# Mamba's ramp and drain: output weights rounded later, fewer idle matmuls, early choice in three parts, last y ahead of scoring

## What is computed

```python
x = x + attention(layernorm(x))          # 16 heads, sliding window of 128
x = x + moe(layernorm(x), gate, w1, w2)  # 8 experts, 2 of them for each row
x = x + mamba(layernorm(x))              # inner width 1024, 16 heads, state 128
x = x + moe(layernorm(x), gate, w1, w2)

def mamba(x):                            # the stage that is changed
    z, xBC, dt = split(x @ in_proj_w.T)
    xs, B, C = split(silu(causal_conv4(xBC) + conv_b))
    y = scan(xs * dt, A, B, C) + xs * D  # state carried over blocks of 64 rows
    y = y * silu(z)
    return (y / sqrt(mean(y * y) + 1e-5) * norm_w) @ out_proj_w.T

def moe(x):
    two best of softmax(x @ gate.T), renormalised; sum of silu(x @ g) * (x @ u) @ w2 over them
```

## Time and profile before

| | |
|---|---|
| times of three runs | 1614.23, 1621.25 and 1623.17 us, median 1621.25 us |
| profiled execution, its time and its span | 1608.78 us, 1607.1 us |
| PE busy in the span | 93%, at a mean granted clock of 0.972 |
| DVE, ACT, POOL busy | 57%, 45%, 38% |
| Mamba's first and last matmul | 738.78 us; 1304.38 us (a group of 1.88 us) |

### The profile page before, as it was taken

How to read it: one execution, slowest core, us unless ns; L and a number is a source line. 1 busy time by engine, 2 the same in 40 slices (tenths; PEclk the granted TensorE clock), 3 DMA queues, 4 the chain that set the end, 5 groups by cost and what they waited for, 6 DMA issues and landing times. The chain is left out here.

```text
span 1607.1 us, 34125 instructions
## 1 busy us (share of the span) xinstructions
PE 1493.9 (93%) x11983; PEld 1262.4 (79%) x12004; DVE 923.4 (57%) x2133; ACT 721.0 (45%) x1784; POOL 606.0 (38%) x473
## 2 busy tenths in 40 slices
PE   6999999999699999997799999999999779999996
PEld 5787887887478898895588787887887558999996
DVE  4677677776732234223687978878878762222221
ACT  3766666666222234333555644564546302333332
POOL 5655465465323334431222332233223403333342
PEclk9999999999799999998899999999999969999999
DMA  6364454463569877543001011010100138787753
GB/s 218 105 206 163 175 204 149 177 210 138 206 210 329 242 221 225 125 67 106 14 21 34 21 34 54 21 34 21 43 32 21 35 130 270 218 266 204 190 97 49
DMA packets 95917, 212.36 MB, mean 132 GB/s; under 512 B 7216, under 2 KB 7216, under 8 KB 94512
## 3 DMA queue, kind: packets, MB, share of 16 engines
q1 hardware_dynamic: 76736, 166.58, 29.7%
q0 software_dynamic: 17472, 40.90, 12.8%
q10 hardware_dynamic: 1584, 3.15, 0.5%
HBM read 136.94 MB, written 73.66 MB: 131 GB/s over the span
## 5 line engine op out<-in xcount | busy, mean ns | idle before, releaser
L1299 PE MATMUL bank<-ring,halves 128*128 x1872 | 332.0, 326 | 3.5 <-ACT halves L1139 3.5
L1299 PEld LDWEIGHTS bank<-ring,halves 128*128 128x128 f32 x1872 | 302.6, 188 | 10.6 <-issue 4.5
L499 POOL TENSOR_TENSOR arena<-arena 128x1024 f32<-128x1024 f32 x64 | 123.8, 1934 | 142.2 <-DVE arena L579 140.6
L1697 DVE SCALAR_TENSOR_TENSOR arena<-arena 128x256 f32<-128x256 f32 x240 | 128.4, 577 | 19.3 <-ACT arena L1916 16.5
L1593 POOL TENSOR_TENSOR arena<-arena 128x1024 f32<-128x1024 f32 x16 | 31.3, 1957 | 280.1 <-ACT arena L1970 240.8
L792 PE MATMUL bank<-arena 128*128 128x128 f32 x1024 | 125.0, 281 | 1.8 <-ACT arena L692 0.8
L711 ACT ACTIVATE arena<-arena 128x256 f32<-128x256 f32 x256 | 126.3, 499 | 0.0
L792 PEld LDWEIGHTS bank<-arena 128*128 128x128 f32 x1024 | 119.0, 195 | 7.7 <-issue 3.6
L1119 POOL DMA_INDIRECT out_dram<-arena x39 | 61.7, 1582 | 154.2 <-issue 90.8
L1119 POOL DMA_INDIRECT mid_rows<-arena x39 | 61.8, 1585 | 148.2 <-issue 94.3
L1139 ACT ACTIVATE halves<-bank 128x512 fp32r<-128x512 f32 x78 | 46.6, 597 | 157.2 <-PE bank L1282 157.2
(11 more groups left out here) (285 smaller groups left out, 3265.8 us busy)
## 6 DMA issues: line engine op xcount, KB each, us to landing
ring<-expert_halves SPq DMA_DIRECT2D x16, 4352.0 KB, 18.8
expert_halves<-expert_high SPq DMA_DIRECT2D x16, 1088.0 KB, 8.7
expert_halves<-expert_rest SPq DMA_DIRECT2D x16, 1088.0 KB, 10.8
arena<-in_w_dram SPq DMA_DIRECT2D x8, 1088.0 KB, 6.6
normalised_rows<-arena SPq DMA_DIRECT2D x33, 256.0 KB, 2.0
arena<-in_x_dram SPq DMA_DIRECT2D x32, 256.0 KB, 2.7
arena<-mid_rows SPq DMA_DIRECT2D x32, 256.0 KB, 2.8
w_in_raw<-in_in_w_dram SPq DMA_DIRECT2D x16, 290.0 KB, 6.6
```

Of the source, the lines that this page charges most:

```text
L499: nc.gpsimd.tensor_tensor(held, held, spread(rinv[:, HG * g:HG * g + HG], 2, 2 * P), ALU.mult)\
L1299: last = nc.tensor.matmul(bank[1 + 2 * par + part][:, 0:INTER], rows_parts[a][:, par, k * P:k * P + P], weights(at, b, (2 * k + part) * IN ...
L1697: last = nc.vector.scalar_tensor_tensor(out=slot[:, j], in0=cin[:, c, k:k + PAIR], scalar=taps[:, c, k:k + 1], in1=slot[:, j], op0=ALU.mul ...
```

## The change

Six edits, all of them in the order of work:

- TensorE's idle matmuls ahead of Mamba are 19 where they were 26; in the prologue ScalarE copies the fifth unit in ahead of the silu of the third.
- ScalarE makes the eight high parts of the output weights in turn 0 behind `conv_in(1, 0)`, no longer ahead of the turn; VectorE makes their rests behind `convolve(1, 0)`, no longer ahead of `own_out(0)`.
- `early_choice` is three calls, for tiles 0 to 5, 6 to 11, and 12 and 13. In Mamba they stand in the last turn behind `rest_of_y(13)`, behind `first_block(14)` and behind `rest_of_y(14)`. In attention all three stand where the one stood.
- In the last tile VectorE's work has an order of its own, `last_rows`: the y of tile 15 is made before tile 14 is scored.
- Tile 14's normalised rows get memory of their own (`keep_apart`), so that the y of tile 15 may be rounded first. The scoring products of tiles 14 and 15 both come behind the last projection on TensorE, in banks 1 and 2.
- 12 new idle matmuls stand between `early_rank` and `turn_y(15)`; the two halves of `spots` stand on either side of the last `put_out`.

```diff
     def early_rank(self, pe):
-        pe.wait_ge(self.early_both, 1)
+        pe.wait_ge(self.early_both, len(self.CHOICES) - 1)
...
         scored = Scoring(core, sem, xn_rows, scored_rows_at, scored_at)
+        scored.keep_apart(TILES - 2, xc_at)
...
+                if not front:
+                    dve.wait_ge(x_turned, TILES)
+                    sort.early_choice(link, 0)
                 mix(t)
                 first_block(t)
+                if not front:
+                    sort.early_choice(link, 1)
                 second_block(t)
-                if first:
-                    rest_of_w_out()
...
                 if front:
                     convolve(link, n, 0)
+                if first:
+                    rest_of_w_out()
...
+            def last_rows(link, t):
+                dve.wait_ge(scored.ready, t - 1)
+                sort.early_choice(link, 2)
+                mix(t)
+                first_block(t)
+                second_block(t)
+                put_out(t - 1)
+                own_out(t)
+                rows_done(link, t, 1)
+                dve.wait_ge(added, t)
+                scored.statistics(dve, link, xres)
+                scored.normalise(dve, t - 1, xres)
+                mean_of(t)
+                rest_of_y(t)
+                dve.wait_ge(z_made, 2 * TILES)
+                sort.early_spots(dve, link)
+                sort.spots(0, sort.EARLY, 0)
+                put_out(t)
+                dve.wait_ge(added, TILES)
+                scored.statistics(dve, link, xres)
+                scored.normalise(dve, t, xres)
+                scored.logits_out(dve, t - 1, bank[1])
+                last = sort.spots(0, sort.EARLY, 1)
+                scored.logits_out(dve, t, bank[2])
+                link(last)
...
                 act.wait_ge(y_turned, t + 1)
                 after(act, out_made, t)
-                after(act, scored.made, t)
-                after(act, scored.stored, 16 * t)
+                after(act, scored.made, min(t, TILES - 2))
+                after(act, scored.stored, 16 * min(t, TILES - 2))
...
                 if front:
                     conv_in(n, 0)
+                if not begun:
+                    high_of_w_out()
...
-            stay_busy(core, bank[7], 26)
+            stay_busy(core, bank[7], 19)
...
             sort.early_rank(pe)
+            stay_busy(core, bank[1], 12)
             turn_y(TILES - 1)
             project_high(TILES - 1)
             project_rest(TILES - 1)
-            pe.wait_ge(scored.xn_ready, TILES)
-            scored.turn(pe, TILES - 1, bank[7])
-            scored.product(pe, TILES - 1, bank[7])
+            scored.turn(pe, TILES - 2, bank[1])
+            scored.product(pe, TILES - 2, bank[1])
+            scored.turn(pe, TILES - 1, bank[2])
+            scored.product(pe, TILES - 1, bank[2])
```

More of the change, by code:

```diff
@@ L199, in __init__, with own_rows, keep_apart, xn @@
         self.made, self.ready, self.stored = sem("logits_made"), sem("logits_ready"), sem("out_xn_stored")
+    def own_rows(self, at):
+        xn, at = cut(self.core.arena, at, D)
+        return xn, cut(self.core.arena, at, KD, P)[0]
+    def keep_apart(self, n, rows_at):
+        self.apart, self.rows_apart = n, self.own_rows(rows_at)
+    def xn(self, n):
+        return (self.rows_apart if isinstance(n, int) and n == self.apart else self.own)[0]
+    def xnT(self, n):
+        return (self.rows_apart if isinstance(n, int) and n == self.apart else self.own)[1]
     def statistics(self, dve, link, x):
@@ L238, in product @@
         for k in range(KD):
-            last = self.nc.tensor.matmul(bank[:, 0:EXPERTS], self.xnT[:, k], self.core.gate[:, k],
+            last = self.nc.tensor.matmul(bank[:, 0:EXPERTS], self.xnT(n)[:, k], self.core.gate[:, k],
                                          start=(k == 0), stop=(k == KD - 1))
@@ L615, in step @@
                     dve.wait_ge(made, SORT_MADE)
-                    sort.early_choice(link)
+                    for part in range(3):
+                        sort.early_choice(link, part)
                 if front:
@@ L1422, in mamba @@
         bc.append(c)
+    xc_at = at
     xc, at = cut(arena, at, KY, PAIR)
@@ L1833, in turn @@
                 rest_of_y(t - 1)
+                if not front:
+                    last_rows(link, t)
+                    return
                 mix(t)
                 first_block(t)
-                if front:
-                    convolve(link, n, 2)
+                convolve(link, n, 2)
                 second_block(t)
-                if front:
-                    convolve(link, n, 3)
-                else:
-                    dve.wait_ge(z_made, 2 * TILES)
-                    sort.early_choice(link)
+                convolve(link, n, 3)
                 put_out(t - 1)
@@ L1876, in _ @@
                 turn(link, i, i % 2, first=(i == 0), front=(i < LAST))
-            sort.early_spots(dve, link)
-            mean_of(TILES - 1)
-            rest_of_y(TILES - 1)
-            for k in range(TOPK):
-                last = sort.spots(0, sort.EARLY, k)
-            link(last)
-            put_out(TILES - 1)
-            dve.wait_ge(added, TILES)
-            scored.statistics(dve, link, xres)
-            scored.normalise(dve, TILES - 1, xres)
-            scored.logits_out(dve, TILES - 1, bank[7])
         @block.scalar
@@ L1993, in decay, with high_of_w_out @@
                     last.then_inc(decays_ready, 1)
+            def high_of_w_out():
+                act.wait_ge(w_out_here, 16)
+                for k in range(KY):
+                    nc.scalar.activation(w_out_parts[0][:, k], w_out[:, k], ACT.Copy, scale=norm[:, k:k + 1])\
+                        .then_inc(w_out_high, 1)
             def turn(i, pp):
@@ L2054, in _ @@
             conv_in(0, 3)
+            conv_in(0, 4)
             conv_out(0, 2, 0)
-            conv_in(0, 4)
             conv_out(0, 3, 0)
```

43 lines of the change are left out of this document (20 added, 23 removed).

## The result

| | before | changed |
|---|---|---|
| median of 12 runs of each, taken beside one another | 1614.09 us | 1603.89 us |
| span of the profiled execution | 1607.1 us | 1605.1 us |
| busy: PE, DVE, ACT, POOL | 93, 57, 45, 38% | 93, 58, 45, 38% |
| mean granted clock | 0.972 | 0.972 |
| Mamba, from its first load to the mixture's first load | 569.34 us | 558.91 us |

The ratio is 0.992, with a 95% interval from 0.9901 to 0.9939. That is 12.9 us less (9.8 to 16.0); the forecast was 17.0 less. The ratio is not the quotient of the two medians in the table, which lie 10.2 us apart (0.9937); that value is inside the interval too.

The account below looks back on a forecast made before the run. TensorE, busy nearly all the time, was taken as the bound, so only its waits and low clock could pay. Terms -1.5 - 6.4 - 9.2 + 0.1 = -17.0 us took 1621.25 to 1604.3 us; range 1596 to 1611.

Parts of the forecast that it names:

- Idle matmuls: Ahead of Mamba: seven fewer idle matmuls on TensorE let the first turning start earlier, -1.5 us.
- Ramp: Turn 0 into tile 1: moving high parts and rests brings TensorE to `block_states(1)` earlier, -6.4 us carried.
- Without that wait the clock should hold: Turn 0, behind the 5.16 us wait ahead of `raw_steps`: matmul groups there shrink by some 1.2 us.
- the new place of the fifth `conv_in`: Prologue on ScalarE: put at nothing, since `gate(0, 0)` waits for the last silu; without that cover, 1.3 us.
- my first rival: Turn 0: the clock still falls, `from_states` and `raw_steps` at half speed cost 3.4 us; 1607.7 us, chance 0.20.
- The step that TensorE can't be over 6.9 us ahead at `block_states(1)`: Tile 1: ScalarE, delayed by the moved high parts, ends `decay` later, so TensorE waits and is only 6.9 earlier.
- The drain from `block_states(15)` on: Last turn: earlier last y, warm turning and projection, `spots` split, warm last product; together 10.2 us less.
- Where the parts of the choice go: Mamba's last turn: parts fill VectorE's waits; GpSimd may hold parts 0 and 1, nothing to 3.3 us, taken as +1.0.
- The whole drain: Last turn: -10.2 plus 1.0 for the choice's parts makes -9.2 us; bounds 5 to 10.2.
- Attention: Attention's early choice: three parts are 1.6 us longer but hidden by VectorE's wait; one moved small instruction costs +0.1 us.
- The second (the drain gives half): Last turn: GpSimd holds the choice by 3.3 us, last projection half cold; 4.4 us back, 1608.7 us, chance 0.15.
- The other two: Gain lost before the end to late engines, 1613 or more (0.08); slower, prologue clock falls, near 1630 (0.02).

Follow-up runs that it names:

- ramp alone: The kernel before with only the ramp's edits (19 idle matmuls, prologue order, high parts and rests later): ratio 0.9954, Mamba 562.1 us.
- part 0 moved: The changed kernel with part 0 of Mamba's choice behind `mask_products(14)`, part 1 left behind `first_block(14)`: ratio 0.9901, Mamba 554.5 us.
- best two: "parts moved" plus attention's choice in one call with early `slot_at`, and ScalarE's high parts behind `rows_out(2)` and `rows_out(3)`: ratio 0.9906, Mamba 552.6 us.
- no idle matmuls: "parts moved" without the twelve idle matmuls between `early_rank` and `turn_y(15)`: ratio 0.9929, Mamba 559.9 us.
- one choice: The changed kernel with all 14 tiles chosen in one call behind `second_block(15)`, attention's choice one call too: ratio 0.9941, Mamba 559.7 us.
- parts moved: The changed kernel with parts 0 and 1 of Mamba's choice behind `mask_products(14)` and `mask_products(15)`, where GpSimd is idle: ratio 0.9912, Mamba 553.6 us.
- attention as before: "parts moved" with attention's early choice in one call and `slot_at` made in it, as before the change: ratio 0.9885, Mamba 556.3 us.

## Why the prediction was right or wrong

**The time** came out at 1603.89 us for a forecast of 1604.3, by luck: two errors cancelled. The three runs that I started from had a median of 1621.25; twelve runs of the same kernel beside the changed one had 1614.09. From that base a gain of 17.0 would have given 1597.1. The gain itself was 12.9 by the ratio (10.2 between the medians), and its interval, 9.8 to 16.0, leaves 17.0 out. The base was 7.2 us too high and the gain 4 to 7 too large.

**Idle matmuls**, -1.5: right in sign and size for the matmuls themselves. Nineteen take 5.70 us up to the turning, 753.64 - 747.94, where 26 took 7.90 (738.78 to 746.68): -2.2. The 0.7 beyond the forecast is the clock, which rose sooner behind the start of the stage: from 2 to 4 us behind the first idle matmul it was 0.68, where it was 0.50 before.

**Ramp**, -6.4, with the idle matmuls -7.9: measured -6.9 at `block_states(1)` and -7.2 in the stage (ramp alone), -7.0 in the changed kernel. But steps of it were wrong and cancelled. The step "Without that wait the clock should hold" failed, and so did the new place of the fifth `conv_in`, "put at nothing". Before, TensorE stood 1.01 and 0.55 us ahead of the last two products of z up to `turn_xs(0)`, and the clock held; in the changed kernel it stands once, for 1.84 us, and the clock fell in the group behind that wait. `turn_xs(0)`, on which `xs_out(0)` hangs, started 4.45 us behind the start of that group. In "part 0 moved", where the clock held behind the same wait, it was 2.89:

```profile
775.35 2.12 PE L2158 MATMUL bank<-w_in_high,halves 128*128 128x512 f32 x8 [1.85 <-ACT arena L1968]
```

That is 1.6 us. The clock fell a second time behind the wait of 2.38 us ahead of `own_rows(0)`, whose 64 small matmuls took 3.45 us and not 2.08; 0.9 of this counts, since with the warm one TensorE waits 0.42 us for VectorE behind it. So my first rival came true in the changed kernel, and so did one of my signs of being wrong, a ramp's clock below 1.00 behind 745. In the ramps with these edits the clock was below 1.00 from 32 to 40 us behind the stage's start in nine of twelve, and at 1.00 in both kernels with the old ramp, in which it fell later. No run has only one of the edits in the prologue, so which of them brings this is not shown.

The step that TensorE can't be over 6.9 us ahead at `block_states(1)`, since ScalarE's high parts hold it, was too strict. In two executions, "part 0 moved" and "best two", the clock stayed at 1.00 from 8 us on through the ramp; in the first of them, with the high parts in their new place, `block_states(1)` came at 77.1, 8.8 us earlier than before and not 7.9.

**The drain from `block_states(15)` on**, -10.2: measured 38.8 - 29.0 = 9.8. The y, its turning, the projection at full speed and the order of `spots` and the addition went as worked out. The twelve idle matmuls earn their place (no idle matmuls, one choice).

**Where the parts of the choice go**, +1.0: this is the step that failed. At `block_states(15)` 0.7 us were left of 7.0. The middle turns take 0.4 of that in the ramp-alone version too, so the parts and the clock behind them took 5.9: 2.15 us up to the product of tile 13, and 3.7 behind it.

The first piece is shown. Part 0 was held for (1.55 - 0.17) + (1.98 - 0.33) = 3.0 us and part 1 for 0.60 - 0.17 = 0.4, together a little more than my upper end of 3.3 for both. Of this 2.15 us reached the product of tile 13, against the version with the parts moved; most of the rest is made up by `mix(14)`, which is itself held there (2.15 us) and isn't behind the choice (1.22). I named the right sign, `mix(14)` late by over 2 us (it was 3.3), but reasoned that a held instruction in a wait is cheap. It is not where the wait is just as long as the instruction unheld: all of the holding sticks out.

The second piece, 3.7 us of low clock, I had not in the sum at all, neither in the term nor in its bounds. But it is the price of the parts only in small part as far as the runs show. Up to `own_rows(15)` the low clock took 3.5 to 4.1 us in the three versions with the lateness, and 2.5 to 3.0 in the seven without it in which the clock fell all the same. So the term that I put at 1.0 cost 5.9 in this execution, of which some 3 can be laid to the parts: 2.15, and 0.8 behind it, which is what the cold product of tile 13 alone lost (1.87 us, not 1.06). The whole drain, put at -9.2 with a lower bound of 5, came to -3.9 in this execution.

The rule of the Trainium skill, "SBUF — State Buffer", section "SBUF: two separate sides", priced it better than I did: 3.3 us held, the whole instruction waited for. The trace agrees: both held pieces end as a GpSimd instruction ends. I had read it too narrowly, for instructions with two SBUF inputs. It names as well those in a mode that uses both ports. The cast and `slot_at`, with one input each, were held for 1.4 and 1.1 us; whether they run in such a mode no run here shows. My count of instructions at risk left them out.

**Attention**, +0.1: by VectorE's own row +0.9, of which between nothing and all reaches the barrier.

**Rivals.** The first (the clock falls in the ramp) happened; it cost some 2.5 us, 1.6 ahead of `turn_xs(0)` and 0.9 around `own_rows(0)`, where the rival had 3.4 in `from_states` and `raw_steps`. The second (the drain gives half) is nearest to what came: right on the holding, wrong on the place of the cold work, which was behind tile 13 and not in the last projection. The other two did not happen. One rival came true, another in part, and the time still fell on the forecast: the time alone says little here.

**What stays open.** How much of the 3.7 us of low clock the lateness owes. In the eleven versions without a wait of over half a microsecond ahead of turning tile 13 (before included) the time to `own_rows(15)` was 16.0 us in four and 18.5 to 19.0 in seven; in the three with such a wait 19.5 to 20.1. Each version has one profile, and three of three against seven of eleven doesn't show that the wait makes the clock fall; it shows only that the clock fell earlier there, ahead of the product and not behind it. The same code shows both: "attention as before" has Mamba exactly as "parts moved", with the same waits up to there, and yet

```profile
1259.38 1.97 PE L2181 MATMUL bank<-ident,arena 128*128 128x128 f32 x8
1261.15 1.65 PE L2188 MATMUL bank<-ident,arena 128*128 128x128 f32 x8
...
1268.34 2.96 PE L2239 MATMUL bank<-arena 64*128 64x512 f32 x8 [1.96 <-ACT arena L2025]
```

So the 553.6 us of "parts moved" was a fortunate execution; 556 is the commoner value, and the gain that the better places promise is nearer 3 us than 5.3. The ratios, 0.9885 to 0.9914 against 0.992, fit either.

## What to carry to other kernels

A wait of VectorE is free room only if GpSimd is idle in it: where GpSimd runs 1.9 us passes, a 0.2 us instruction put in the wait can last 1.5, so look at GpSimd's timeline at the very place, and put small work where it stands still, even if VectorE is busy there. Price a new wait on TensorE by itself and by the low clock that may stand behind it, and look in other executions whether the clock falls there without the wait: here it did in seven of eleven, and most of the 3.7 us could not be laid to the wait. And take a forecast's base from as many runs as its gain needs: three runs were off by 7 us for a gain of 13.

## What the runs showed of the hardware

TensorE's granted clock fell with no longer wait in front of it than the 0.69 us that stand ahead of the scoring product in every version (and 0.43 in "part 0 moved"). The product of tile 13 (128x8) and the groups behind it (128x16 and 128x64) are very small, 2.4 us in all; the clock fell among them or right behind, and the transposes that follow ran at 1.04 to 1.10 us for eight in some executions and at 1.65 to 1.97 in others of the same code. The Trainium skill, "TensorE: Matmul & The Clock Gate", Part 1, says that the number of slow matmuls at a kernel's start differs from run to run of one kernel; the traces show the like in the middle of one.

Holding goes both ways. In "parts moved", `mix(14)` began 1.07 us before GpSimd's L1620 ended and took 2.15 us and not 1.22; L1624, which began while it ran, took 2.89 us and not 1.90.

Seven idle matmuls fewer did not cost the clock at the start of the ramp: in all twelve versions with 19 of them the granted clock was between 0.88 and 1.00 from 4 to 8 us behind the stage's start. In one of these, "parts moved", it then fell, to 0.70 from 8 to 12 us, and `block_states(1)` was no later for it, since its clock held from 32 to 40 us, where the clock of nine others fell.
